# Two transformer layers on one core: layer 1's key mask is added by VectorE instead of TensorE

## The reference, cut to what matters

```python
# layer 1
xn = _ln(x, ln_w, ln_b)
q = xn @ Wq + bq
k = xn @ Wk + bk + (1.0 - src_mask) * -1000000.0      # src_mask: one value per position
q = softmax(q.reshape(b, t, h, dh), axis=-1)
k = softmax(k.reshape(b, t, h, dh), axis=1)           # over the positions
v = ((xn @ Wv + bv) * src_mask).reshape(b, t, h, dh)
att = einsum('bnhd,bnhl->bhdl', k, v)
y = einsum('bnhd,bhdl->bnhl', q, att).reshape(b, t, d)
hh = _ln(y, ln2_w, ln2_b) * (1.0 + scale) + shift
return x + silu(hh) @ W_out + b_out
```

## Time and profile before

| | |
|---|---|
| runs | 1108.95, 1110.1, 1110.1 us, median 1110.1 |
| profiled execution | 1106.18 us, of which the span of the instructions is 1104.4 |
| TensorE busy | 1055.1 us (96%), 8696 products |
| weight loads | 910.7 us (82%) |
| VectorE | 759.8 us (69%) |
| ScalarE | 591.9 us (54%) |
| GpSimd | 449.2 us (41%) |
| mean granted TensorE clock | 0.989 of full speed |
| DMA | 71.65 MB, mean 65 GB/s |

### The profile page before, as it was taken

How to read it: one execution, slowest core, us unless ns; L and a number is a source line. 1 busy time by engine, 2 the same in 40 slices (tenths; PEclk the granted TensorE clock), 3 DMA queues, 4 the chain that set the end, 5 groups by cost and what they waited for, 6 DMA issues and landing times. The chain is left out here.

```text
span 1104.4 us, 25954 instructions
## 1 busy us (share of the span) xinstructions
PE 1055.1 (96%) x8696; PEld 910.7 (82%) x8696; DVE 759.8 (69%) x1326; ACT 591.9 (54%) x1960; POOL 449.2 (41%) x783
## 2 busy tenths in 40 slices
PE   4899999999999999999999999999999999999995
PEld 3678888888888888888887778888888888888884
DVE  4556666766667666676568777777777777777764
ACT  4264677766777667776597544333434434333431
POOL 3232343343433434334333444444444444444432
PEclk9998999999999999999999999999999999999997
DMA  7743102111021110111102201111111111111111
GB/s 211 231 168 118 61 25 62 62 40 59 24 62 62 40 59 24 62 62 41 61 25 97 82 28 46 58 59 57 57 57 57 57 57 57 47 47 35 41 39 57
DMA packets 46017, 71.65 MB, mean 65 GB/s; under 512 B 10256, under 2 KB 14448, under 8 KB 45968
## 3 DMA queue, kind: packets, MB, share of 16 engines
q1 hardware_dynamic: 45968, 71.02, 20.1%
HBM read 54.19 MB, written 16.79 MB: 64 GB/s over the span
## 5 line engine op out<-in xcount | busy, mean ns | idle before, releaser
L1267 PE MATMUL bank<-xt_hi,w_hi 128*128 128x256 f32 x768 | 227.9, 297 | 0.5 <-DVE w_lo L828 0.5
L449 POOL TENSOR_SCALAR stat<-stat 128x1 f32<-128x1 f32 x128 | 34.5, 270 | 454.5 <-DVE stat L877 428.2
L1268 PE MATMUL bank<-xt_lo,w_hi 128*128 128x256 f32 x768 | 218.2, 284 | 0.0
L1269 PE MATMUL bank<-xt_hi,w_lo 128*128 128x256 f32 x768 | 218.0, 284 | 0.0
L607 ACT ACTIVATE prob<-prob,neg_max 128x128 f32<-128x128 f32 x512 | 198.5, 395 | 5.9 <-DVE neg_max L900 5.9
L626 ACT ACTIVATE th<-z_s 128x512 f32<-128x512 f32 x64 | 40.5, 632 | 249.5 <-POOL z_s L483 249.4
L1267 PE MATMUL bank<-w_hi,xt_hi 128*128 128x512 f32 x384 | 157.9, 411 | 1.0 <-DVE w_lo L828 1.0
L1267 PEld LDWEIGHTS bank<-xt_hi,w_hi 128*128 128x128 f32 x768 | 148.7, 194 | 5.5 <-DVE w_lo L828 2.0
L1269 PE MATMUL bank<-w_hi,xt_lo 128*128 128x512 f32 x384 | 150.5, 392 | 0.0
L1268 PE MATMUL bank<-w_lo,xt_hi 128*128 128x512 f32 x384 | 149.8, 390 | 0.0
L1268 PEld LDWEIGHTS bank<-xt_lo,w_hi 128*128 128x128 f32 x768 | 148.2, 193 | 0.0
(11 more groups left out here) (130 smaller groups left out, 2205.7 us busy)
## 6 DMA issues: line engine op xcount, KB each, us to landing
x_in<-in_x_dram SPq DMA_DIRECT2D x32, 256.0 KB, 2.8
x_res<-in_x_dram SPq DMA_DIRECT2D x32, 256.0 KB, 2.9
between_layers<-x_res SPq DMA_DIRECT2D x32, 256.0 KB, 2.0
x_in<-between_layers SPq DMA_DIRECT2D x32, 256.0 KB, 2.8
x_res<-between_layers SPq DMA_DIRECT2D x32, 256.0 KB, 2.7
out_dram<-x_res SPq DMA_DIRECT2D x32, 256.0 KB, 2.5
room<-in_L_cond_W_emb_dram SPq DMA_DIRECT2D x8, 512.0 KB, 5.7
prob<-in_L_cond_emb_w_dram SPq DMA_DIRECT2D x4, 512.0 KB, 7.8
```

What stands on the lines that cost most here:

```text
L449: pool.tensor_scalar(v[:, 8:9], v[:, 7:8], EPS, None, ALU.add).then_inc(s[a_in].sem, 1)
L1267: pe.matmul(o, a_hi, b_hi, start=start, stop=False)
L1268: pe.matmul(o, a_hi, b_lo, start=False, stop=False)
L1269: return pe.matmul(o, a_lo, b_hi, start=False, stop=stop)
```

## The change

The mask's row of layer 1 goes to DRAM like that of layer 0 (`mask_bias[1]`), without being cut in parts. For each pair SyncE loads it broadcast to all partitions into `mask_pair` (128 x 256, f32). The products with `ones_parts` are gone, and so are `mask_parts`, `mask_wide`, `ones_parts`, their memsets and moves. Layer 1's keys are taken out of the bank by VectorE, at the head of `k_soft`, in two instructions that add bias and mask; ScalarE's `k_out` remains for layer 0. In the mixed step `k_soft(f, slot, 0)` moves from behind the second sequence's softmax to before `stats1(n, 0)`. `consts` is posted by the addition that makes `pick`. SyncE waits for both layers' mask rows (`mask_cut` 4, `mask_saved` 32).

```diff
@@ SyncE
             def load_mask(f, b):
-                sp.wait_ge(mask_saved, 16)
+                sp.wait_ge(mask_saved, 32)
                 sp.wait_ge(*done(s["masked3"], f + (b - 2)))
...
+            def load_mask_pair(f):
+                sp.wait_ge(*done(s["kb_out"], f + (-GROUP)))
+                at = f + (-B)
+                flat = mask_bias[1].rearrange("(o b) p -> o (b p)", o=1)
+                row = (flat[:, at.const * P:at.const * P + N] if at.reg is None
+                       else flat[:, bass.ds(at.value() * P, N)])
+                sp.dma_start(mask_pair[:], row.broadcast_to([P, N])).then_inc(s["mask_pair_in"].sem, 16)
...
@@ SyncE, start
-                sp.wait_ge(mask_cut, 2)
-                sp.dma_start(mask_bias, mask_tmp[0][:, P:2 * P]).then_inc(mask_saved, 16)
+                sp.wait_ge(mask_cut, 4)
+                for l in range(2):
+                    sp.dma_start(mask_bias[l], mask_tmp[l][:, P:2 * P]).then_inc(mask_saved, 16)
...
-                sp.wait_ge(mask_cut, 8)
-                for j, row in enumerate(PART_ROWS):
-                    sp.dma_start(mask_wide[row:row + 1, :].rearrange("o (b n) -> o b n", b=B),
-                                 mask_parts[:, j, :]).then_inc(mask_moved, 16)
@@ SyncE, steps: step 14 (before layer 1's WQ is loaded), step_mixed, step1
+                load_mask_pair(n)
@@ GpSimd
-            pool.memset(ones_parts[:], 0.0).then_inc(once, 1)
-            pool.wait_ge(once, 5)
-            for r0 in PART_ROWS:
-                last = pool.memset(ones_parts[r0:r0 + 1, :], 1.0)
-            last.then_inc(once, 1)
-            pool.wait_ge(once, 6)
-            pool.tensor_tensor(pick[:], ident[:, 0:2 * B], ident[:, 2 * B:4 * B], ALU.add).then_inc(once, 1)
-            pool.wait_ge(once, 7)
-            pool.memset(mask_wide[:], 0.0).then_inc(consts, 1)
+            pool.wait_ge(once, 4)
+            pool.tensor_tensor(pick[:], ident[:, 0:2 * B], ident[:, 2 * B:4 * B], ALU.add).then_inc(consts, 1)
@@ ScalarE, step_mixed and step1
-                k_out(1, f, slot, 0)
...
-                k_out(1, f, slot, 1)
@@ VectorE
             def k_soft(f, slot, pair):
-                dve.wait_ge(*done(s["ka_out" if pair == 0 else "kb_out"], f))
+                if pair == 0:
+                    dve.wait_ge(s["mask_pair_in"].sem, (f + (-B)).value() * (16 // GROUP) + 16)
+                out = s["ka_out" if pair == 0 else "kb_out"]
+                dve.wait_ge(*done(s["ka_pe" if pair == 0 else "kb_pe"], f))
+                dve.wait_ge(*done(s["qk_pe"], f + (-GROUP - 1)))
+                from_bank = bank[SECOND["K"][pair]][:].rearrange("p (c n) -> p c n", c=2)
+                kv = chunks(k_exp[:, slot, :])
+                for j in range(2):
+                    c = 2 * pair + j
+                    last = dve.scalar_tensor_tensor(out=kv[:, c, :], in0=from_bank[:, j, :], scalar=col[:, 1, KB, c:c + 1],
+                                                    in1=mask_pair[:], op0=ALU.add, op1=ALU.add)
+                last.then_inc(out.sem, GROUP)
+                dve.wait_ge(*done(out, f))
...
@@ VectorE, step_mixed
                 softmax(k, 0, (3,))
+                dve.wait_ge(bias_dve, TURN[1, WK])
+                k_soft(f, slot, 0)
                 stats1(n, 0)
                 softmax(k, 1, (0, 1, 2))
                 output(FIRST, late + (-1), 1)
                 softmax(k, 1, (3,))
-                k_soft(f, slot, 0)
                 k_soft(f, slot, 1)
@@ TensorE, project
-                    if l == 1:
-                        at = f + (-B)
-                        cols = (mask_wide[:, at.const * P:at.const * P + N] if at.reg is None
-                                else mask_wide[:, bass.ds(at.value() * P, N)])
-                        pe.matmul(o, ones_parts[:], cols, start=True, stop=False)
...
@@ TensorE, step_mixed
-                pe.wait_ge(mask_moved, 16 * len(PART_ROWS))
```

More of the change, by code:

```diff
@@ L7 @@
 F32R = mybir.dt.float32r
-BF16 = mybir.dt.bfloat16
 ALU = mybir.AluOpType
@@ L16 @@
 MASKED = -1000000.0
-PART_ROWS = (0, 32, 64)
 class At:
@@ L79, in build @@
     WQ, WK, WV, WO = range(4)
-    mask_bias = nc.dram_tensor("mask_bias", [B, P], F32, kind="Internal").ap()
+    mask_bias = [nc.dram_tensor(f"mask_bias{l}", [B, P], F32, kind="Internal").ap() for l in range(2)]
     middle = nc.dram_tensor("between_layers", [B, T, D], F32, kind="Internal").ap()
@@ L113, in build @@
         silu_cond = film_ab[:, 1].rearrange("p i c b -> p (i c b)").rearrange("p (k b) -> p k b", k=KE)
-        mask_parts = sb("mask_parts", [B, 3, P], BF16)
         mask_row = sb("mask_row", [P, GROUP, P])
-        mask_wide = sb("mask_wide", [P, B * P], BF16)
-        ones_parts = sb("ones_parts", [P, P], BF16)
+        mask_pair = sb("mask_pair", [P, N])
         mask_col = sb("mask_col", [P, 2 * B])
@@ L196, in build @@
         cond_in, cond_act, cond_pe, cond_dve = (sem(f"cond_{n}") for n in ("in", "act", "pe", "dve"))
-        mask_in, mask_cut, mask_saved, mask_moved, mask_pe, mask_ready = (
-            sem(f"mask_{n}") for n in ("in", "cut", "saved", "moved", "pe", "ready"))
+        mask_in, mask_cut, mask_saved, mask_pe, mask_ready = (
+            sem(f"mask_{n}") for n in ("in", "cut", "saved", "pe", "ready"))
         norm_in = [sem(f"norm_in{l}") for l in range(2)]
@@ L228, in build @@
             s[n] = [Stage(sem(f"{n}{b}")) for b in range(GROUP)]
+        s["mask_pair_in"] = Stage(sem("mask_pair_in"), B)
         src = [t["x"], middle]
@@ L411, in step1 @@
                     load_back(1, k, 1)
+                if n:
+                    load_mask_pair(n)
+                if k:
                     store(1, k, 0)
@@ L589, in q_out, with k_out @@
                 last.then_inc(s["pa_out" if pair == 0 else "pb_out"].sem, GROUP)
-            def k_out(l, f, slot, pair):
+            def k_out(f, slot, pair):
                 act.wait_ge(*done(s["ka_pe" if pair == 0 else "kb_pe"], f))
                 act.wait_ge(*done(s["qk_pe"], f + (-GROUP - 1)))
-                from_bank = bank[(FIRST, SECOND)[l]["K"][pair]][:].rearrange("p (c n) -> p c n", c=2)
-                kv = chunks((k_t, k_exp)[l][:, slot, :])
+                from_bank = bank[FIRST["K"][pair]][:].rearrange("p (c n) -> p c n", c=2)
+                kv = chunks(k_t[:, slot, :])
                 for j in range(2):
                     c = 2 * pair + j
-                    last = act.activation(kv[:, c, :], from_bank[:, j, :], ACT.Identity, bias=col[:, l, KB, c:c + 1])
+                    last = act.activation(kv[:, c, :], from_bank[:, j, :], ACT.Identity, bias=col[:, 0, KB, c:c + 1])
                 last.then_inc(s["ka_out" if pair == 0 else "kb_out"].sem, GROUP)
@@ L673, in start @@
                 act.wait_ge(bias_dve, 2)
-                k_out(0, f, 0, 0)
-                k_out(0, f, 0, 1)
+                k_out(f, 0, 0)
+                k_out(f, 0, 1)
                 for b in range(GROUP):
@@ L700, in step0 @@
                 y_t_out(k, 0)
-                k_out(0, f, slot, 0)
+                k_out(f, slot, 0)
                 prob_turned(k, 1, (0,))
@@ L705, in step0 @@
                 exps(k, 1, (3,))
-                k_out(0, f, slot, 1)
+                k_out(f, slot, 1)
                 if i == G - 2:
@@ L1276, in project @@
                     o = bank[to][:, j * N:(j + 1) * N]
-                    if l == 1:
-                        at = f + (-B)
-                        cols = (mask_wide[:, at.const * P:at.const * P + N] if at.reg is None
-                                else mask_wide[:, bass.ds(at.value() * P, N)])
-                        pe.matmul(o, ones_parts[:], cols, start=True, stop=False)
                     for kc in range(C):
                         last = three(o, hi[l][w][:, kc, c * P:(c + 1) * P], lo[l][w][:, kc, c * P:(c + 1) * P],
-                                     xt_hi[:, slot, kc, :], xt_lo[:, slot, kc, :], kc == 0 and l == 0, kc == C - 1)
+                                     xt_hi[:, slot, kc, :], xt_lo[:, slot, kc, :], kc == 0, kc == C - 1)
                 last.then_inc(s[sm].sem, GROUP)
```

20 lines of the change are left out of this document (3 added, 17 removed).

## The result

| | before | after |
|---|---|---|
| median, us | 1109.88 (1107.08 to 1110.30, 6 runs) | 1122.09 (1119.46 to 1124.62, 6 runs) |
| profiled execution, its span | 1106.18, 1104.4 | 1120.31, 1118.5 |
| products on TensorE | 8696 | 8632 |

The change makes the kernel 1.1% slower: ratio 1.0114, 95% interval 1.0092 to 1.0136. Forecast were 1118.9 us, in a range of 1109.5 to 1122; the time lies 0.1 us above that range. The profiled execution of before is faster than all six of its runs, and that of after is the second fastest of six; so the two traces differ by 14.1 us where the medians differ by 12.2.

A forecast was written before the change was run, and what follows sets the result against it. It took layer 1 to be bound by a ring of engine waits as long as TensorE's work. Start -4.2, mixed step +1.1, step 16 -0.4 and loop +12.3 gave +8.8 on 1110.1: 1118.9 us, range 1109.5 to 1122.

The forecast's parts named there:

- a ring of VectorE, GpSimd and ScalarE: Layer 1: wait chain from `query` through y_s, norms, z_s and s_lo to `output`; vector part 18.65 us, TensorE part 11.3.
- a collision with L981: Layer 1: shifted by 0.85 us, GpSimd's z_s would wait behind VectorE's L981; 0.43 us a step, bounds 0 and 0.57.
- the loop's term: Layer 1, steps 17 to 30: 0.85 - 0.40 + 0.43 = 0.88 us a step, 12.3 us in all.
- The new loads ... Nothing: SyncE's queue: one 128 KB mask load a pair, little behind it, DMA engines 18% busy; no cost.
- The pair in the ring: Second `k_soft` in layer 1: two added VectorE instructions delay GpSimd's release by 0.85 us, bounds 0.78 to 0.94.
- Rival B: Layer 1: no collision with L981, 0.45 us a step, total +2.8, 1112.9 us; chance 25%.
- The products: TensorE's part of layer 1's ring: four removed products a step save 0.40 us together, 0.48 at most.
- The count: The loop's cost applies in steps 17 to 30 of layer 1, 14 steps.
- The mixed step: Step 15: VectorE empties bank 7 late, so TensorE stalls 1.1 us before `weigh(k, 0)`; bounds 0 and 1.5.
- The start: Kernel's start: `consts` posted earlier, without the memsets before it, gains 4.2 us; bounds 3.5 and 4.4.
- The cover of the first `k_soft`: Layer 1, ahead of y_s: VectorE waits for TensorE there, so the first pair is free, 0.13 us left at worst.
- Rival C: Layer 1: added work hidden, TensorE the only bound, 0.40 us gained in 15 steps; 1099.9 us, chance 10%.

The follow-up runs named there:

- experiment 3: The single run const_scalar: changed kernel with the number 1.0 in place of the keys' bias column in the new instructions; 1122.47 us.
- const_scalar: Changed kernel with the number 1.0 in place of the keys' bias column in the new VectorE instructions; 1122.47 us, layer 1 step 30.91 us.
- no_lock_first: Changed kernel, query maximum's subtraction reading the bank instead of SBUF, for each pair's first sequence only; 1114.39 us, step 30.52 us.
- before_both: Kernel before, with constants posted early and the next pair's statistics ahead of the second `k_soft`; 1101.54 us, ratio 0.9912 to the kernel before.
- late_soft: reorder_mixed with layer 1's second `k_soft` one place later, behind the second sequence's `y_norm`; 1098.77 us, ratio 0.9895 to the kernel before.
- mask_early: Changed kernel with the first mask load for a layer 1 pair issued some 30 us earlier, in step 14; 1123.24 us, mixed step 40.24 us.
- dve_first_half: Changed kernel with the second half of layer 1's keys taken out by ScalarE again, without mask, VectorE keeping the first; 1098.86 us, step 29.50.
- reorder: Changed kernel with the next pair's second statistics moved ahead of the second `k_soft` in layer 1; 1105.29 us, ratio 0.9969 to the kernel before.
- reorder_mixed: reorder with the mixed step's second `k_soft` also moved, right behind the first, ahead of the softmax; 1102.53 us, ratio 0.9947 to the kernel before.

## Where the prediction was right, and which steps of it failed

The time was outside the range, and too low was the sum: +8.8 forecast, +12.2 in the medians, +14.1 in the profiled spans. The mechanism was as forecast: the new pair sits in a ring of VectorE, GpSimd and ScalarE that was as long as TensorE's work; s_lo stands 0.14 us ahead of the late `output` as before; the products' removal is felt only in TensorE's part of the ring; a collision with L981 comes on top.

Two steps failed. The first is the loop's term, 0.85 - 0.40 + 0.43 = 0.88 us a step and 12.3 in all, which measured 1.14 a step and 14.8 in all, mostly because the new pair of instructions was priced too low. The second is "The new loads ... Nothing": it, with the bank's late emptying, made the mixed step cost 2.2 us where 1.1 were forecast. These two misses, 2.5 and 1.1 us, less 0.3 elsewhere in layer 1, make up nearly all of the 3.4 us by which the medians lie above the sum. Term by term:

- **The pair in the ring**: forecast 0.85, measured 1.02. The instruction takes 480 ns, not 417, and experiment 3 shows why: the column, 60 ns. Neither instruction of the earlier trace rows has a column as its scalar (L866 has the number 1.0; the `col` in its row is its second tensor), so the line through them priced another form than the one added. The maximum's wait adds 0.09 (702.62 less 701.65 + 0.88). The pair of 0.97 lies above the bounds of 0.78 to 0.94. Of the last 0.05, 0.02 are one late norm, in pair 19 (+10.08); the rest I did not take apart.
- **The collision**: forecast 0.43 on z_s, measured 0.50 on the norm. That the price came near while another instruction paid it is partly luck. L981 did keep its place, +9.88 us after y_s in both traces (708.34 less 698.46; 708.88 less 699.00). But the norm moved to +9.80, not to 8.84 + 0.85 = +9.69, and so L981 came at the norm's own start and not 0.19 behind it. The forecast form was seen in const_scalar. Rival B (no collision) is refuted in this kernel, and what it would give was measured as no_lock_first, 30.52 us a step.
- **The products**: forecast 0.40, measured 0.37 in TensorE's part of the ring, and 0.39 between before_both and late_soft.
- **The count**: the ring is closed between pair 17 and pair 30, 13 times, not 14. Pair 30's step has no statistics of a next pair, costs 0.11 and no more. By luck this error made up for 0.9 us of the step that was put too short.
- **The mixed step**: forecast 1.1 (bounds 0 and 1.5), measured 2.2. The bank's late emptying is half of it, as forecast: with the load out of the way (mask_early) the step is 1.1 us longer than before. The other half is the sentence that failed outright, "The new loads ... Nothing": in step 14 the mask's load stands ahead of two loads of 512 KB of weights and of x_in, x_in lands 1 us late for VectorE, and everything behind moves. I had looked at the mean DMA share and at the loop, not at what stands behind the load in this one step. The two costs lean on each other: where ScalarE still empties the bank (dve_first_half) VectorE waits 0.89 us for x_in, but the mixed step takes 39.71 us, only 0.6 more than before.
- **The start**: forecast -4.2 (bounds 3.5 and 4.4), measured -4.1 at TensorE's first instruction and -2.3 in pair 14 of these two traces. The second number compares an early start of the kernel before with an ordinary one of the kernel after. In the medians, if the rest of each execution goes as in its trace (2.2 - 0.5 + 14.8 - 0.2 = 16.3), +12.2 leaves -4.1 for the start. That is an estimate; it agrees with the forecast, and no run shows it by itself.
- **The cover of the first `k_soft`**: right. y_s still waits for TensorE, 0.47 and 1.02 us, and the first pair costs 0.05.

Rival C (TensorE the only bound) is refuted: the vector part grew and the step with it. It needs another order, and late_soft comes within some 0.1 us a step of it.

The Trainium skill ("SBUF — State Buffer", the section on SBUF's two sides) says that VectorE with two SBUF inputs and a GpSimd instruction that reads SBUF exclude each other for a whole instruction. The norm's 1.27 us beside L978, and its 0.77 once L978 has one SBUF input, agree. So does the norm at 702.22, which lasts 0.77 us though the new pair runs from 701.65 to 702.53. "Whoever starts first" doesn't come out of the recorded starts: in the step shown the norm's stands 0.08 us ahead of L978's, and it was the norm that waited; the same holds in every second step, with 0.07 to 0.09.

## What to carry to other kernels

When an engine is busy for 99.5% of a step, look also at what its last wait ends on: if a result arrives 0.15 us before it is used, in every step, the chain through the other engines is just as long, and work moved onto that chain costs its full price while the work taken off the busy engine brings little. A busy share can hide such a wait, as it hid 0.3 us a step here; the distance between two starts, compared with a step in which nothing waits, shows it. The remedy is then the order, not the engine: the same instructions behind the last one that the chain needs cost 0.1 us (a step of 29.28 in place of 31.02). And of a new load ask what stands behind it in its queue at the one place where much is loaded, not how busy the queue is on average.

## What the runs showed of the hardware

- A scalar_tensor_tensor of 128x256 out of a bank with one SBUF input takes 480 ns with a column as its scalar and 420 ns with a number.
- Where a VectorE instruction with two SBUF inputs (0.69 us) meets two GpSimd instructions that follow each other (0.77 and 1.05 us), who pays depends on tenths of a microsecond. Arriving from 0.27 us before the first one's start to 0.09 after it, it holds up the first (1.06 to 1.32 us); from 0.17 to 0.20 after, and at 0.64 (once each in reorder and reorder_mixed), it runs next and holds up the second (1.48 to 1.50); from 0.73 on, VectorE itself waits (0.94 to 1.60). The price is 0.3 to 0.55 us for GpSimd in the first two cases, none in the third. Nothing was seen between 0.20 and 0.64.
- A load of 128 KB, one row broadcast to 128 partitions, took 5.5 us to land just ahead of the weights (two loads of 512 KB), and with it there they took 6.8 in place of 4.2 us; some 30 us earlier, in a quiet stretch, it took 3.1 us.
- From the start of four transposes to the start of the products that read s_lo pass 0.36 us where s_lo ended 0.23 us before the second (late_soft, pair 17) and 0.75 us where it ended 0.15 before (the kernel before, pair 18); the profile shows TensorE without idle time in both.
